# Moving the first tile's normalization, its projection and half of its matmuls into the stream of weight transposes

## The reference, cut to what matters

```python
xn = (x - mean) / sqrt(var + 1e-5)                      # over the 2048 features
a = tanh(xn @ Wa.T + ba);  b = tanh(xn @ Wb.T + bb)     # 64 states
h_t = a_t * h_{t-1} + b_t                               # scan over 4096 steps
scale = mean(abs(weight))                               # weight: 2048 x 2048
w_t = clip(round(weight / scale), -1, 1)
y = x + (xn + h @ Wout.T + bout) + (xn @ (w_t * scale).T + bias)
```

## Time and profile before

| | |
|---|---|
| time, median of 3 runs | 741.6 us |
| time of the profiled execution | 742.53 us |
| its span (core 7, the slowest; core 0 has 736.7) | 741.0 us |
| TensorE busy | 590.1 us, 80% |
| VectorE busy | 348.9 us, 47% |
| ScalarE busy | 235.8 us, 32% |
| GpSimd busy | 215.2 us, 29% |
| granted TensorE clock, core 7 | 0.996 |

### The profile page before, as it was taken

One profiled execution on the slowest core, in us unless ns is written; L12 is line 12 of the kernel. 1 busy time (PEld: TensorE's weight loads), 2 busy tenths in 40 slices (PEclk: granted clock), 3 DMA queues, 4 the chain that ended last, 5 costly groups with the idle time before them and its releaser, 6 DMA issues.

```text
span 741.0 us, 11300 instructions; the slowest of 8 cores (736.7 to 741.0 us)
## 1 busy us (share of the span) xinstructions
PE 590.1 (80%) x3804; PEld 311.9 (42%) x3804; DVE 348.9 (47%) x303; ACT 235.8 (32%) x250; POOL 215.2 (29%) x742
## 2 busy tenths in 40 slices
PE   0111314554999999999999999999999999999995
PEld 0111314442444444445444444444444454444442
DVE  0000099982344455554555554444465544555521
ACT  0654515554214222222333222332222223332220
POOL 0000012265223333333343433333333333433310
PEclk9999999999999999999999999999999999999998
DMA  7998128751133333333333333333333333233321
GB/s 222 337 341 293 28 73 272 280 171 58 37 108 138 142 143 117 115 115 115 115 114 115 115 114 121 137 135 142 142 120 114 115 114 115 115 114 115 114 92 79
DMA packets 16831, 103.02 MB, mean 139 GB/s; under 512 B 4326, under 2 KB 4358, under 8 KB 4358
## 3 DMA queue, kind: packets, MB, share of 16 engines
q1 hardware_dynamic: 9350, 51.96, 21.5%
q0 software_dynamic: 7424, 50.34, 17.7%
HBM read 68.73 MB, written 33.55 MB: 138 GB/s over the span
## 4 chain that ended last, share of the span: by engine, by line
PE 66%; DMA 8%; ACT 8%; DVEq 4%; DVE 4%; ACTq 3%; issue 3%; POOL 1%; POOLq 1%; SPq 1%
PE pffn L515 15%; PE pffn L518 15%; PE pffn L530 15%; PE pffn L526 15%; DMA vv<-wf 8%; ACT xnT L298 4%; DVE wbn L364 3%; ACTq L297 3%; PE pab L503 3%; PE ptr L540 2%; DVEq L363 2%; DVEq L358 2%; ACT xnT L294 1%; POOL wocv L582 1%; ACT xnT L207 1%
## 5 line engine op out<-in xcount | busy, mean ns | idle before, releaser
L515 PE MATMUL pffn<-w_rhs,xnT 128*128 128x512 bf16 x512 | 194.7, 380 | 0.0
L518 PE MATMUL pffn<-w_rhs,xnT 128*128 128x512 bf16 x512 | 194.6, 380 | 0.0
L526 PE MATMUL pffn<-w_rhs,xnT 128*128 128x512 bf16 x512 | 194.0, 379 | 0.0
L530 PE MATMUL pffn<-w_rhs,xnT 128*128 128x512 bf16 x512 | 194.0, 379 | 0.0
L342 DVE TENSOR_REDUCE sums<-sx 128x1 f32<-128x2048 f32 x32 | 73.1, 2286 | 173.7 <-DMA sx<-x 173.4
L276 ACT ACTIVATE xnb<-sx,nmr,yr 128x2048 bf16<-128x2048 f32 x31 | 65.0, 2097 | 127.5 <-POOLq L627 127.5
L294 ACT COPY xnT<-ptr 128x1024 bf16<-128x1024 bf16 x31 | 31.4, 1013 | 217.8 <-PE ptr L540 217.8
L393 DVE SCALAR_TENSOR_TENSOR outb<-pffn,negs,vv 128x1024 f32<-128x1024 f32 x32 | 41.1, 1284 | 90.3 <-PE pffn L556 75.4
L593 POOL TENSOR_SCALAR mm_<-sums 128x1 f32<-128x1 f32 x32 | 8.3, 258 | 236.8 <-DVE sqscr L344 233.7
L526 PEld LDWEIGHTS pffn<-w_rhs,xnT 128*128 128x128 bf16 x512 | 50.1, 98 | 60.4
L530 PEld LDWEIGHTS pffn<-w_rhs,xnT 128*128 128x128 bf16 x512 | 50.1, 98 | 60.4
(11 more groups left out here) (101 smaller groups left out, 564.1 us busy)
## 6 DMA issues: line engine op xcount, KB each, us to landing
sx<-x SPq DMA_DIRECT2D x32, 1024.0 KB, 6.3
y<-outb POOLq DMA_DIRECT2D x32, 1024.0 KB, 5.6
outb<-wf POOLq DMA_DIRECT2D x11, 1024.0 KB, 6.8
wtile<-wf SPq DMA_DIRECT2D x8, 1024.0 KB, 11.4
vv<-wf SPq DMA_DIRECT2D x8, 1024.0 KB, 13.5
sqscr<-wf POOLq DMA_DIRECT2D x5, 1024.0 KB, 6.8
wasb<-wa SPq DMA_DIRECT2D x1, 512.0 KB
wosb<-wout SPq DMA_DIRECT2D x1, 512.0 KB, 17.4
```

The source lines that it names most:

```text
L515: tensor.matmul(pffn[:, 0:512], lhs, w_rhs[:, 2048 * c:2048 * c + 512], start=st_, stop=False)
L518: tensor.matmul(pffn[:, 512:1024], lhs, w_rhs[:, 2048 * c + 512:2048 * c + 1024], start=st_, stop=False)
L526: tensor.matmul(pffn[:, 1024:1536], lhs, w_rhs[:, 2048 * c + 1024:2048 * c + 1536], start=st_, stop=False)
L530: ins = tensor.matmul(pffn[:, 1536:2048], lhs, w_rhs[:, 2048 * c + 1536:2048 * c + 2048], start=st_, stop=False)
```

## The change

ScalarE does the normalization of tile 0 ahead of its copies of weight 11, and the two `xnT` copies of tile 0 ahead of its copies of weight 13. TensorE transposes weights 0 to 12, then transposes tile 0, makes its projection, and makes its first 32 main matmuls (output columns 0 to 1023); then it transposes weights 13 to 15, and goes on with the second 32 matmuls. The lists of VectorE, GpSimd and SyncE are untouched, and no operation is added or taken away.

```diff
@@ scalar
             for j in range(NW):
+                if j == 11:
+                    scalar.wait_ge(s_stats, 1)
+                    scalar.drain()
+                    scalar.activation(xnb[:, 0:D], sx[:, 0:D], AF.Identity,
+                                      bias=nmr[:, 0:1], scale=yr[:, 0:1]
+                                      ).then_inc(s_xnbs, 1)
+                if j == 13:
+                    scalar.wait_ge(s_tr, 1)
+                    scalar.drain()
+                    scalar.copy(xnT[:, 0:1024], ptr[:, 0:1024]
+                                ).then_inc(s_xnT, 1)
+                    scalar.wait_ge(s_tr, 2)
+                    scalar.drain()
+                    scalar.copy(xnT[:, 1024:2048], ptr[:, 1024:2048]
+                                ).then_inc(s_xnT, 1)
                 for grp in range(2):
                     scalar.wait_ge(s_wtr, 2 * j + grp + 1)
...
-            scalar.wait_ge(s_stats, 1)
...
-            scalar.copy(xnT[:, 1024:2048], ptr[:, 1024:2048]).then_inc(s_xnT, 1)
@@ tensor
-            for j in range(NW):
+            def wtr(j):
...
+                    elif j == 13:
+                        tensor.wait_ge(s_wtrc, 2 * 12 + grp + 1)
+                        tensor.wait_ge(s_xnT, 2)
                     else:
                         tensor.wait_ge(s_wtrc, 2 * (j - 1) + grp + 1)
...
-            tensor.wait_ge(s_wtrc, 32)
+            for j in range(13):
+                wtr(j)
+            tensor.wait_ge(s_wtrc, 26)
             tensor.wait_ge(s_xnbs, 1)
...
+            tensor.wait_ge(s_xnT, 1)
+            tensor.matmul(pab[:, :], babr[:, :], sonr[:, :],
+                          start=True, stop=False)
...
+            tensor.wait_ge(s_wtrc, 16)
+            for c in range(NCH):
...
+                tensor.matmul(pffn[:, 0:512], lhs,
+                              w_rhs[:, 2048 * c:2048 * c + 512],
+                              start=st_, stop=False)
+                tensor.matmul(pffn[:, 512:1024], lhs,
+                              w_rhs[:, 2048 * c + 512:2048 * c + 1024],
+                              start=st_, stop=False)
+            for j in range(13, NW):
+                wtr(j)
             for k in range(NT):
...
                 if k == 0:
                     tensor.wait_ge(s_wtrc, 32)
                 else:
                     tensor.wait_ge(s_ev, 2 * k)
```

More of the change, by code:

```diff
@@ L487, in _ @@
             ins.then_inc(s_tr, 1)
+            tensor.wait_ge(s_bab, 1)
+            tensor.wait_ge(s_wabcp, 2)
+            tensor.wait_ge(s_small, N_SMALL)
+            tensor.wait_ge(s_xnT, 1)
+            tensor.matmul(pab[:, :], babr[:, :], sonr[:, :],
+                          start=True, stop=False)
+            for c in range(NCH):
+                if c == 8:
+                    tensor.wait_ge(s_xnT, 2)
+                ins = tensor.matmul(pab[:, :], wab[:, 128 * c:128 * (c + 1)],
+                                    xnT[:, 128 * c:128 * (c + 1)],
+                                    start=False, stop=(c == NCH - 1))
+            ins.then_inc(s_ab, 1)
+            tensor.wait_ge(s_wtrc, 16)
+            for c in range(NCH):
+                st_ = (c == 0)
+                lhs = xnT[:, 128 * c:128 * (c + 1)]
+                tensor.matmul(pffn[:, 0:512], lhs,
[6 more added lines that the diff above has]
+                wtr(j)
             for k in range(NT):
@@ L492, in _ @@
                     tensor.wait_ge(s_tanh, 2 * k)
[L493 to L507, removed]
+                    tensor.wait_ge(s_xnT, 2 * k + 1)
+                    tensor.matmul(pab[:, :], babr[:, :], sonr[:, :],
+                                  start=True, stop=False)
+                    for c in range(NCH):
+                        if c == 8:
+                            tensor.wait_ge(s_xnT, 2 * k + 2)
+                        ins = tensor.matmul(
+                            pab[:, :], wab[:, 128 * c:128 * (c + 1)],
+                            xnT[:, xo + 128 * c:xo + 128 * (c + 1)],
+                            start=False, stop=(c == NCH - 1))
+                    ins.then_inc(s_ab, 1)
+                    tensor.wait_ge(s_ev, 2 * k - 1)
+                    for c in range(NCH):
+                        st_ = (c == 0)
+                        lhs = xnT[:, xo + 128 * c:xo + 128 * (c + 1)]
+                        tensor.matmul(pffn[:, 0:512],
+                                      lhs, w_rhs[:, 2048 * c:2048 * c + 512],
+                                      start=st_, stop=False)
+                        tensor.matmul(pffn[:, 512:1024], lhs,
+                                      w_rhs[:, 2048 * c + 512:2048 * c + 1024],
+                                      start=st_, stop=False)
                 if k == 0:
@@ L510, in _ @@
                 else:
[L511 to L521, removed]
                     tensor.wait_ge(s_ev, 2 * k)
```

## The result

The changed kernel takes 756.0 us (median of 9 runs), beside 742.4 us for the kernel before (10 runs in the same comparison). The ratio is 1.0178, with a 95% interval of 1.0163 to 1.0192: 13.2 us slower. The forecast was 754.0 us against 741.6, +12.4 us, range 750 to 758. The profiled executions took 755.39 and 742.53 us, +12.9.

What follows compares the result with a forecast made beforehand. The prediction took TensorE to bound the loop, VectorE the weight stage, and GpSimd's late statistics the hole between. Terms -0.97 + 4.49 + 7.36 + 1.5 gave +12.4 us, 754.0 us against 741.6, range 750 to 758.

Steps and rivals of the forecast that it cites:

- Step 1: Ahead of weight 11's copies, ScalarE waits some 24 us for GpSimd's statistics of tile 0; normalization at 173.09.
- The 0.97 us from the absent `g_sb`: VectorE's `g_sb` of weight 15 no longer slows a GpSimd tiny transfer, so normalization starts 0.97 us earlier; bounds 0 and 3.8.
- The 2.82 us gap: GpSimd without work between the tiny transfers and tile 0's statistics chain; kept, though it might shrink with neighbours idle.
- rival B: Smaller loss: clock stays up, first half loses nothing, GpSimd's 2.82 gap shrinks; +6.8 to +10.9, 748.4 to 752.5; 13%.
- Step 2: Weights 11 and 12 are copied after the normalization, +4.49 us; tile 0's transposes start at 179.82, before 176.30.
- Step 3: Tile 0's transposes, projection and first 32 matmuls take 12.11 us as before, ending at 191.93; -1.3 to 0, taken 0.
- Step 4: Weights 13 to 15 lie between tile 0's halves: six ScalarE copies in 6.46 us, 7.36 with first copy and handover.
- Step 5: Tile 0's second 32 matmuls: 6.91 us plus 1.5 for TensorE starting at the 1.2 GHz clock; bounds 0 and 6.9.
- Step 6: Late load of x tile 2 delays VectorE's sums, eviction of tile 0 hidden by 1.5 us: 0, upper end +2.3.
- Sum: -0.97 + 4.49 (weights 11 and 12) + 7.36 (weights 13 to 15) + 1.5 (clock) = +12.4 us.
- Rival A: Faster: statistics come before ScalarE reaches its wait; -11 to -5 us, 730.7 to 736.6; 2%.

Runs made afterwards that it cites:

- experiment 1: Changed kernel with GpSimd's 16 tiny bias transfers moved to the head of its list: 750.6 us, ratio 1.0102.
- experiment 2: Kernel before with GpSimd's bias transfers moved to the head of its list: 739.4 us, ratio 0.9952.
- experiment 3: Changed kernel with early bias transfers and statistics of tiles 0 and 1 in pieces between weight loads, with drains: 778.2 us, ratio 1.0475.
- experiment 4: Kernel before with early bias transfers, statistics in pieces between weight loads with drains, and normalization ahead of weight 11's copies: 781.2 us, ratio 1.0521.
- experiment 5: Changed kernel with early bias transfers and early statistics in pieces between weight loads, on semaphores instead of drains: 749.6 us, ratio 1.0092.
- experiment 9: Changed kernel with ScalarE's normalization of tile 0 ahead of weight 13's copies instead of weight 11's: 750.4 us, ratio 1.0116.
- experiment 8: Changed kernel with two unused 512-column matmuls behind each transpose group of weights 13 to 15: 754.1 us, ratio 1.0152.
- experiment 10: Changed kernel with VectorE's sums of tiles 0 and 1 at its start, GpSimd's bias transfers and statistics before its first load: 723.6 us, ratio 0.9753.
- experiment 7: Changed kernel with TensorE's old order and ScalarE's two tile 0 copies behind its last weight copy; normalization kept early: 755.8 us, ratio 1.0178.
- experiment 11: Kernel before with early sums, statistics and bias transfers, and normalization ahead of weight 11's copies; TensorE's order as before: 727.2 us, ratio 0.9808.
- experiment 12: Kernel before with early sums and statistics, tile 0 prepared before the first weight block, its matmuls woven between weights: 710.1 us, ratio 0.9577.

## Why the prediction was right, step by step

- **Step 1, the gate.** Right. ScalarE waited 24.32 us (24.3 to 25.2 on the eight cores), where the forecast has 173.09 - 148.74 = 24.35; that the normalization also came at 173.10 is luck in part, since over the cores it starts at 170.1 to 173.1. The 0.97 us from the absent `g_sb` is there: 8.61 us for the 16 transfers instead of 9.61. The order of the lists was enough to see it.
- **The 2.82 us gap** was kept, rightly, but I did not know what it was and let it range from 2.82 to 0. It is 2.82 in the changed kernel too, where VectorE is idle during all of it, so it is not owed to neighbours (this part of rival B is refuted). Experiments 1 to 4, with 5 beside them, show a drain that waits for transfers in flight, about 7 us behind a weight load; that the 2.82 us behind the tiny ones is the same thing fits their landing (median 2.6 us in the kernel before), but was not tested by itself. The expectations of experiments 1 and 2 were too good by 3.0 and 2.5 us for it, in the second together with the slower chain.
- **Step 2, weights 11 and 12**: tile 0's transposes at 179.91, forecast 179.82. Experiment 9 takes the two weights off: -4.6 us in time for a term of 4.49 less the 0.97 that comes back, 3.5. Its trace moves by 3.2 (59.6 to 56.4).
- **Step 3, the first half**: 192.05 - 179.91 = 12.14 us, forecast 12.11.
- **Step 4, weights 13 to 15**: six copies in 6.72 us (192.79 to 199.51), forecast 6.46. With the first copy and the handover the stage took 7.55 us (192.05 to 199.60), forecast 7.36. Of the 0.26, one half lies at 194.89 to 195.11, where the granted clock was 1.00, and only the other in handovers at the lower clock; with the clock held up (experiment 8) the six took 6.56 us.
- **Step 5, the clock**: the loss is 8.73 - 6.91 = 1.8 us, forecast 1.5; over the eight cores it is 1.3 to 1.8. With 0.16 in step 4 the clock costs 2.0, and experiment 8 gives back 1.9 in time and in the trace. The 1.5 was a choice between bounds of 0 and 6.9, not worked out, so its nearness is luck in part: in experiment 10 the same stretch lost 3 us. The rule of the Trainium skill cited there (page "TensorE: Matmul & The Clock Gate", section "Part 4: PE-mode transpose"), that transposes don't count like matmuls for the clock, agrees with the fall inside 196 to 197 us amid transposes; it is not shown by that alone, since TensorE was also idle for much of the time.
- **Step 6, the late x load**: VectorE's sums of tile 2 ended at 206.9 and its eviction of tile 0 began at 209.98 after 3.06 us of idleness, released by TensorE. Nothing late, as taken, and with 3.06 us to spare instead of the 1.5 forecast: the load of x tile 2, issued at 197.15, let the sums start 5.28 us later and not 6.23.
- **Sum**: +12.4 forecast, +12.9 in the profiled executions, +13.2 in the medians. In distance it is 12.97 against 12.38; of the 0.6 us over, 0.3 lie in the second half, 0.2 in the copies of weights 13 to 15 and 0.1 ahead of them.
- **Rival A**, the open gate, could not happen in this list; when the list was changed so that it did (experiments 10 and 5), it gave -10.5 and -10.0 us in distance, near the fast end of its -11 to -5. The reason for the loss is therefore not that the work was moved but what was moved past what: five weights behind a wait whose giver was still 24 us away in another engine's list. Experiment 7 shows that the order on TensorE is neutral in the net, within some 1.5 us, as long as the gate stands; with the clock held up it would be some 1.7 us ahead (754.1 against 755.8 us, experiments 8 and 7; their intervals overlap a little).

## What to carry to other kernels

Before a wait is moved forward in one engine's list, find the instruction that satisfies it in the giver's list and read what stands ahead of it there; a wait that was free at the end of a stage puts everything behind it on that path. An idle hole is filled from its cause: here it was the statistics of two tiles, on engines that had nothing to do. Made early, the sums of tile 0 ended at 17.1 us instead of 98.3 and its statistics at 35.5 instead of 173.9 (core 5 of experiment 10). With TensorE's old order this took 14.8 us off (experiment 11), some 8 of them by emptying the weight stage; the changed order on top was worth 3.6, and everything of tile 0 ahead of and between the weights 17 (experiment 12 against 11). So the order of the matmuls was worth as much as the statistics, but only once these were there. And a kernel whose hole comes from GpSimd is not mended by putting small operations between its transfers: the drains and VectorE's own operations make them long.

## What the runs showed of the hardware that I had not expected

- A drain on GpSimd waits for the transfers that GpSimd has issued: 6.93 and 7.16 us behind a 1 MB load (0.04 us in experiment 5, where no drain stands between), and within 0.04 to 0.06 us of the landing in three places of one trace.
- An operation of GpSimd on 128x1 takes 0.2 us alone (0.39 for the divide) and 2.2 to 2.5 when it starts early beside `wbn`, which reads two SBUF tensors, not only beside the 1.29 us `g_sb`. The Trainium skill (page "SBUF — State Buffer", section "SBUF: two separate sides") describes an exclusive lock on a port pair that VectorE and GpSimd share, held for a whole instruction, also for a VectorE operation with two SBUF inputs; the trace agrees, with these numbers.
- The profile's granted clock shows the fall to 0.50 in the changed kernel, but 1.00 ahead of the first rise, where the matmuls also stood 0.43 us apart. The distance between starts is the safer reading.
